# A transformer block with convolutional attention on one core: six PSUM banks for the first three rows of scores of a batch, and a first stage put in the order of its needs

## The reference

```python
x = x + conv_attn(group_norm(x))        # q, k, v = W @ x + b; softmax(q.T k) applied to v; gamma * out + x * se(x)
t = tokens(x)
a = layer_norm(t)
t = t + softmax(a @ a.T) @ a            # second attention
t = t + moe(layer_norm(t))              # 8 experts, the 2 best of a router's softmax
```

## Time and profile before

| | us |
|---|---|
| median of 3 runs (lowest to highest) | 2839.08 (2837.59 to 2839.95) |
| the profiled execution | 2836.02 |
| its span | 2834.2 |
| PE busy, matmuls | 2636.5 (93%) |
| DVE busy | 2161.3 (76%) |
| ACT busy | 2023.1 (71%) |
| POOL busy | 446.9 (16%) |
| one maximum of a chunk (DVE, L818), mean of 720 | 0.633 |

### The profile page before, as it was taken

One profiled execution on the slowest core, in us unless ns is written; L12 is line 12 of the kernel. 1 busy time (PEld: TensorE's weight loads), 2 busy tenths in 40 slices (PEclk: granted clock), 3 DMA queues, 4 the chain that ended last, 5 costly groups with the idle time before them and its releaser, 6 DMA issues.

```text
span 2834.2 us, 45738 instructions
## 1 busy us (share of the span) xinstructions
PE 2636.5 (93%) x15334; PEld 2381.2 (84%) x15334; DVE 2161.3 (76%) x5499; ACT 2023.1 (71%) x4305; POOL 446.9 (16%) x840
## 2 busy tenths in 40 slices
PE   5999989999899998999989999999999999999996
PEld 4888978889788897889978898888988889888895
DVE  4886778787787877877778777887777877788775
ACT  2777767677676876768767687676867768677774
POOL 0000210032100331003200133001220022200223
PEclk7999999999999999999999999999999999999997
DMA  1000000000000000000000000000000000000000
GB/s 35 1 1 18 7 6 1 18 7 6 7 1 18 7 6 7 1 18 7 9 4 1 18 7 11 2 1 18 10 9 1 1 21 6 9 1 1 4 9 12
DMA packets 10037, 23.05 MB, mean 8 GB/s; under 512 B 1992, under 2 KB 8528, under 8 KB 8784
## 3 DMA queue, kind: packets, MB, share of 16 engines
q1 hardware_dynamic: 9808, 20.14, 2.0%
HBM read 10.70 MB, written 9.44 MB: 7 GB/s over the span
## 4 chain that ended last, share of the span: by engine, by line
PE 61%; DVE 23%; ACT 9%; issue 5%; POOL 2%; SPq 0%; DMA 0%; ACTq 0%; DVEq 0%; POOLq 0%
PE ps L1005 17%; PE ps L1007 17%; PE ps L1006 17%; PE ps L1018 9%; DVE mx L818 6%; DVE pt_lo L828 3%; DVE pt_lo L902 3%; ACT pt_hi L612 2%; ACT p_rows L600 2%; DVE u_tok L879 1%; ACT p_rows L647 1%; POOL u_rs L518 1%; ACT pt_hi L656 1%; ACT p_rows L681 1%; DVE acc L984 1%
## 5 line engine op out<-in xcount | busy, mean ns | idle before, releaser
L612 ACT ACTIVATE pt_hi<-ps 128x384 fp32r<-128x384 f32 x864 | 425.4, 492 | 319.2 <-PE ps L1018 313.5
L828 DVE TENSOR_TENSOR pt_lo<-ps,pt_hi 128x384 fp32r<-128x384 f32 x864 | 479.5, 556 | 178.7 <-ACT pt_hi L612 170.3
L600 ACT ACTIVATE p_rows<-ps,negmax 128x512 f32<-128x512 f32 (+1 forms) x720 | 464.8, 647 | 72.9 <-DVE negmax L822 65.8
L902 DVE TENSOR_TENSOR pt_lo<-p_rows,pt_hi 128x768 fp32r<-128x768 f32 x432 | 413.9, 959 | 124.1 <-ACT pt_hi L656 122.4
L818 DVE TENSOR_REDUCE mx<-ps 128x1 f32<-128x512 f32 (+1 forms) x720 | 442.0, 633 | 79.4 <-PE ps L1007 55.4
L1018 PE MATMUL ps<-ident,p_rows 128*128 128x128 f32 x2736 | 455.7, 275 | 40.4 <-DVE pt_lo L828 22.9
L647 ACT ACTIVATE p_rows<-ps,shift 128x768 f32<-128x768 f32 x432 | 389.6, 902 | 119.1 <-PE ps L1007 114.0
L1018 PEld LDWEIGHTS ps<-ident,p_rows 128*128 128x128 f32 x2736 | 332.4, 140 | 153.8 <-issue 54.9
L656 ACT ACTIVATE pt_hi<-p_rows 128x768 fp32r<-128x768 f32 x432 | 365.6, 846 | 40.1 <-PE ps L1007 0.7
L1005 PE MATMUL ps<-pt_hi,v_hi 128*128 128x384 f32 x864 | 358.6, 415 | 2.5 <-ACT y_out L621 2.5
L1005 PE MATMUL ps<-xt_hi 128*128 128x384 f32 x864 | 305.2, 353 | 0.0
(11 more groups left out here) (165 smaller groups left out, 5162.4 us busy)
## 6 DMA issues: line engine op xcount, KB each, us to landing
x_chan<-x SPq DMA_DIRECT2D x8, 1152.0 KB, 5.1
y<-y_out SPq DMA_DIRECT2D x48, 192.0 KB, 1.9
p_rows<-ew SPq DMA_DIRECT2D x1, 512.0 KB
p_rows<-eb SPq DMA_DIRECT2D x1, 512.0 KB
p_rows<-wq SPq DMA_DIRECT2D x1, 64.0 KB
p_rows<-wk SPq DMA_DIRECT2D x1, 64.0 KB
p_rows<-wv SPq DMA_DIRECT2D x1, 64.0 KB
w_sb<-w SPq DMA_DIRECT2D x2, 4.0 KB
```

Of the source, the lines that this page charges most:

```text
L600: act.activation(p_rows[:, ROW_BUFFER[r, n % 2], a:a + w], ps[:, c, 0:w], ACT.Exp, bias=negmax[:, r % 2:r % 2 + 1], accum_out=dparts[:, n, ...
L612: act.activation(pt_hi[:, slot, :], ring_bank(step)[:, 0:BW], ACT.Copy)\
L828: dve.tensor_tensor(pt_lo[:, slot, :], ring_bank(step)[:, 0:BW], pt_hi[:, slot, :], ALU.subtract).then_inc(pt_lo_ready, 1)
L902: dve.tensor_tensor(p1_lo[:, w % 3, :], p1_f[:, w % 2, :], p1_hi[:, w % 3, :], ALU.subtract).then_inc(p1_lo_ready, 1)
```

## The change

Scores: in block 0 of each batch the fifteen chunks go round banks 0 to 5, so chunk c of row r is in bank (5 r + c) modulo 6. From block 1 on it is bank c again. Each chunk waits for the Exp that last read its bank; for block 1, row 0 these are chunks 2, 3 and 4 of row 2 (banks 0, 1, 2), chunk 4 of row 1 (bank 3) and chunk 0 of row 2 (bank 4). `pv` of tile 0 waits for chunk 1 of row 2 (bank 5). The maxima get two sets of columns, used by turns. The order of the steps in `attention0` stays as it was.

First stage: x comes in three thirds, each with a semaphore, in every batch. The weights for Q, K and V come in one transfer, the per-channel vectors in one, the two small matrices in one, the expert weights with the router's in one, their biases in one. ACT rounds the three weight matrices, DVE takes the residual behind `gn_mean`. After `gn_var` the normalisation of the first third begins. The squeeze-excite chain, five of the V projections, the folding (now steps `fold` and `foldsplit` in the ring) and the three `base` stand in slots between the scores of block 0 of batch 0. V 0 stands in slot 0, before the first chunk. The staging of the folding moves to other buffers.

```diff
+def score_bank(n, r, c):
+    return (len(QC) * r + c) % 6 if n == 0 else c
+
+def bank_before(n, r, c):
+    if n:
+        i = n * TPB + r - 1
+        if i >= TPB:
+            return i // TPB, i % TPB, c
+        i = max(i for i in range(TPB * len(QC)) if i % 6 == c)
+    else:
+        i = len(QC) * r + c - 6
+    return (0, i // len(QC), i % len(QC)) if i >= 0 else None
...
-def first_stage(b):
-    s = statistics(b) + normalise(b)
-    s += [(step[0], b, step[1]) for slot in sorted(PROJECT_SLOTS) for step in PROJECT_SLOTS[slot]]
-    return s + [step for j in range(NT) for step in attention0(b, 0, j)]
+def first_stage():
+    s = statistics(0)[:9]
+    s += [("xgnorm", 0, 0), ("xg", 0, 0), ("xgnorm", 0, 1), ("kproj", 0, 0), ("xg", 0, 1), ("kproj", 0, 1), ("xgnorm", 0, 2),
+          ("kproj", 0, 2), ("xg", 0, 2), ("qproj", 0, 0), ("kproj", 0, 3), ("kproj", 0, 4), ("kproj", 0, 5)]
+    rest = {1: [("gn_norm", 0)], 2: [("se_in", 0)], 3: [("se_out", 0)], 5: [("fold", 0, 0)], 7: [("fold", 0, 1), ("base", 0, 0)],
+            9: [("fold", 0, 2)], 11: [("foldsplit", 0)], 13: [("base", 0, 1)], 15: [("base", 0, 2)]}
+    merge(rest, {slot: [("vproj", 0, m)] for m, slot in enumerate([0, 2, 4, 8, 12, 16])})
+    merge(rest, {j: attention0(0, 0, j) for j in range(NT)})
+    return s + [step for j in range(NT) for step in rest[j]]
...
+            load(0, 0)
+            sp.dma_start(w_stage[:, :, :], wqkv).then_inc(qkv_loaded, 16)
+            load(0, 1)
+            load(0, 2)
+            sp.dma_start(biases[:, 0:4], channel).then_inc(biases_loaded, 16)
+            sp.dma_start(se_sb[:, :], se).then_inc(se_loaded, 16)
+            sp.dma_start(fold_b, eb).then_inc(fold_loaded, 16)
+            sp.dma_start(fold_w, ew).then_inc(fold_loaded, 16)
...
-            act.wait_ge(w_split, W_SPLITS)
+            act.wait_ge(qkv_loaded, 16)
+            act.activation(w_hi[:, :, :], w_stage, ACT.Copy).then_inc(w_hi_ready, 1)
+            act.wait_ge(biases_loaded, 16)
...
+                elif kind == "foldsplit":
+                    act.wait_ge(bias_folded, 1)
+                    act.activation(rw_pair[:, 0, :], rw_stage, ACT.Copy).then_inc(e_hi_ready, 1)
+                    act.activation(ew_hi[:, :], ew_stage, ACT.Copy).then_inc(e_hi_ready, 1)
...
+                    if not b:
+                        dve.wait_ge(w_hi_ready, 1)
+                        dve.tensor_tensor(w_lo[:, :, :], w_stage, w_hi[:, :, :], ALU.subtract).then_inc(w_lo_ready, 1)
+                        dve.wait_ge(biases_loaded, 16)
+                        dve.tensor_tensor(biases[:, 4:5], biases[:, 2:3], biases[:, 3:4], ALU.mult).then_inc(w_lo_ready, 1)
+                elif kind == "fold":
+                    a, z = FOLD_PARTS[step[2]]
+                    dve.wait_ge(ring_full, filled(step))
+                    dve.tensor_tensor(fold_b[:, a:z], fold_b[:, a:z], ring_bank(step)[:, 0:z - a], ALU.subtract)\
+                        .then_inc(bias_left, 1)
+                elif kind == "foldsplit":
+                    dve.wait_ge(bias_left, len(FOLD_PARTS))
+                    dve.scalar_tensor_tensor(out=fold_w, in0=fold_b, scalar=1.0 / C, in1=fold_w, op0=ALU.mult,
+                                             op1=ALU.add).then_inc(bias_folded, 1)
+                    dve.wait_ge(e_hi_ready, 2)
...
                 elif kind == "xgnorm":
                     u = step[2]
+                    if u == 0:
+                        dve.wait_ge(gn_rstd_ready, at(gn_rstd_ready, "gn_var", b))
...
-                    row = n * TPB + r
-                    if row:
-                        pe.wait_ge(p_rows_ready, at(p_rows_ready, "exp", b, (row - 1) // TPB, (row - 1) % TPB, c))
-                    elif b and c < 4:
+                    before = bank_before(n, r, c)
+                    if before:
+                        pe.wait_ge(p_rows_ready, at(p_rows_ready, "exp", b, *before))
+                    elif b and r == 0 and c < 4:
...
-                    three(ps[:, c, 0:w], q_hi[:, n % 2, tile], q_lo[:, n % 2, tile], k_hi[:, a:a + w],
+                    three(ps[:, score_bank(n, r, c), 0:w], q_hi[:, n % 2, tile], q_lo[:, n % 2, tile], k_hi[:, a:a + w],
...
+                            pe.wait_ge(p_rows_ready, at(p_rows_ready, "exp", b, *bank_before(1, 0, 5)))
```

More of the change, by code:

```diff
@@ L176, in batch @@
     return s
-PLAN = first_stage(0) + [step for b in range(B) for step in batch(b)]
+PLAN = first_stage() + [step for b in range(B) for step in batch(b)]
 RAISES = {
@@ L183 @@
     "se_in": ["ring_full", "se_hidden_ready"], "se_out": ["ring_full", "se_exp_ready"],
+    "fold": ["ring_full", "bias_left"], "foldsplit": ["bias_folded", "e_hi_ready", "e_split"],
     "xgnorm": ["xg_norm_ready"], "xg": ["xg_hi_ready", "xg_lo_ready"], "base": ["base_done"],
@@ L198 @@
 }
[L200 removed]
+LAST = {"fold": "bias_left", "gn_dev": "gn_dev_ready", "gn_var": "gn_var_ready", "se_in": "se_hidden_ready", "se_out": "se_exp_ready",
         "kproj": "k_lo_ready", "vproj": "v_lo_ready", "baset": "base_tok_ready",
@@ L383, in build @@
         y_chan_ready = signal("y_chan_ready")
-        x_loaded = signal("x_loaded")
-        w_loaded = signal("w_loaded")
+        x_loaded = [signal(f"x_loaded{i}") for i in range(LB)]
+        qkv_loaded = signal("qkv_loaded")
+        biases_loaded = signal("biases_loaded")
+        se_loaded = signal("se_loaded")
+        fold_loaded = signal("fold_loaded")
         consts_made = signal("consts_made")
-        column_sums = signal("column_sums")
         bias_left = signal("bias_left")
         bias_folded = signal("bias_folded")
-        w_split = signal("w_split")
+        e_hi_ready = signal("e_hi_ready")
+        e_split = signal("e_split")
+        w_hi_ready = signal("w_hi_ready")
+        w_lo_ready = signal("w_lo_ready")
         vector_chain = signal("vector_chain")
         y_stored = [signal(f"y_stored{i}") for i in range(2)]
-        signals = {s.name: s for s in (base_tok_ready, k_lo_ready, expert_added, terms_ready, gn_dev_ready, gn_var_ready,
+        signals = {s.name: s for s in (base_tok_ready, k_lo_ready, bias_left, expert_added, terms_ready, gn_dev_ready, gn_var_ready,
                                        logit_max_ready, o_added, o1_added, pt_lo_ready, q_lo_ready,
@@ L437, in _, with load @@
         def _(sp):
[L438 to L451, removed]
+            def load(b, u):
+                cols = slice(u * LW, (u + 1) * LW)
+                sp.dma_start(x_chan[:, cols], x[b][:, cols]).then_inc(x_loaded[u], 16)
+            load(0, 0)
[6 more added lines that the diff above has]
+            sp.dma_start(fold_w, ew).then_inc(fold_loaded, 16)
             def store(b, mb):
@@ L459, in _ @@
                     sp.wait_ge(ring_full, filled(("baset", b, NB - 1)))
-                    sp.dma_start(x_chan[:, :], x[b + 1]).then_inc(x_loaded, 16)
+                    for u in range(LB):
+                        load(b + 1, u)
                 if b:
@@ L562, in take @@
                     act.wait_ge(ring_full, filled(step))
+                    if m == 0 and not b:
+                        act.wait_ge(e_split, 2)
                     if m == 0 and b:
@@ L599, in take @@
                         act.wait_ge(ring_full, filled(("pt", b, n - 1, last_tile(c))))
-                    act.activation(p_rows[:, ROW_BUFFER[r, n % 2], a:a + w], ps[:, c, 0:w], ACT.Exp,
+                    act.activation(p_rows[:, ROW_BUFFER[r, n % 2], a:a + w], ps[:, score_bank(n, r, c), 0:w], ACT.Exp,
                                    bias=negmax[:, r % 2:r % 2 + 1],
@@ L702, in _ @@
         def _(dve):
-            dve.wait_ge(w_loaded, 16 * N_WLOADS)
             dve.wait_ge(consts_made, 12)
[L706 to L725, removed]
             def take(step):
@@ L768, in take @@
                     dve.wait_ge(se_exp_ready, at(se_exp_ready, *step))
+                    if not b:
+                        dve.wait_ge(w_lo_ready, 2)
                     link(dve.tensor_scalar(se_tmp, se_e, 1.0, None, ALU.add))
@@ L1036, in take @@
                         .then_inc(ring_full, 1)
+                elif kind == "fold":
+                    a, z = FOLD_PARTS[step[2]]
+                    pe.wait_ge(fold_loaded, 32)
+                    wait_ring(step)
+                    pe.matmul(ring_bank(step)[:, 0:z - a], ones[:, :], fold_w[:, a:z], start=True, stop=True)\
+                        .then_inc(ring_full, 1)
                 elif kind == "se_in":
                     wait_ring(step)
+                    if not b:
+                        pe.wait_ge(se_loaded, 16)
                     pe.wait_ge(se_in_ready, at(se_in_ready, "gn_norm", b))
@@ L1054, in take @@
                     pe.wait_ge(xg_lo_ready, at(xg_lo_ready, "xg", b, m // 2))
+                    if not b and not m:
+                        pe.wait_ge(w_lo_ready, 1)
                     wait_ring(step)
@@ L1153, in take @@
                     m = step[2]
+                    if not b and not m:
```

(1 more changed line is left out.)

54 lines of the change are left out of this document (26 added, 28 removed).

## The result

| | before (with one run more) | after |
|---|---|---|
| median, us (lowest to highest) | 2838.41 (2837.59 to 2839.95) | 2874.0 (2871.69 to 2874.7) |
| ratio to before, 95% interval | | 1.0123 (1.0106 to 1.0141) |
| span of the profiled execution | 2834.2 | 2872.2 |
| granted clock, mean | 0.984 | 0.975 |

The account below looks back on a forecast made before the run. TensorE, busy 36.8 of 38 us from 402 to 440 us, was taken as the bound. Terms -19.3 - 2.3 + 35.6 + 5 = +19 on 2836.0 gave 2855, with 3.1 for the median 2858; range 2841 to 2872.

Parts of the forecast that it names:

- part 5: Clock at the return to five banks: four dips more of 1.3 us, +5 us; bounds -4 to +16.
- Part 1: First stage of batch 0 up to the first scores: scores start at 25.4 us, -29.3 us.
- Part 2: Work put between the rows of batch 0: +10.0 us, leaving -19.3 us for the third row's Exp.
- Part 3: Rows of batches 1 to 7: row 1 gains 0, row 2 gains 0.33 us each, -2.3 us in all.
- The rule that bubbles mean too little PSUM: Skill's rule on bubbles: all sixteen rows 1 and 2 would gain from a sixth bank; trace agreed for batch 0 alone.
- Part 4: Return to five banks at block 1: a circle of chunk, transpose, pt_hi, Exp costs 4.45 us per batch, +35.6 us.
- The fourth rival: Clock falls in every circle: +16 in place of +5, first stage only -14; 2874 us; chance 0.15.
- The first and third rivals: First: the 4.45 us circle is given back, 2818, chance 0.07. Third: sixth bank pays everywhere, 2811, chance 0.03.
- The second: Cover and clock are kind: first stage -23.5, no dip added, circle at 3.3 us; 2840 us; chance 0.10.

Follow-up runs that it names:

- the run with banks in order: Changed kernel with chunk c in bank (c + 3) modulo 5 from block 1 on, order of steps untouched; 2817.2 us, ratio 0.9927.
- the run with the old first stage: Kernel before with the six banks alone, keeping its own loads and first stage; 2897.24 us, ratio 1.0203.
- filler: Changed kernel with useless matmuls in TensorE's idle times, ten before tile 0 and six behind each of tiles 0, 1 and 2; 2842.84 us, ratio 1.0015.
- filler in this gap: Changed kernel with bank (c + 3) modulo 5 from block 1, ten useless matmuls before tile 0 and ten before the store's transpose; 2806.19 us, ratio 0.9886.
- the run with five banks: Changed kernel's new first stage with the five banks of the kernel before; 2819.94 us, ratio 0.9934.
- the Exp first: Changed kernel with the Exp of chunks 2, 3 and 4 of block 0's last row ahead of the first transposed tile; 2842.62 us, ratio 1.0014.
- the run with five banks and filler: New first stage with five banks, plus ten useless matmuls before the store's transpose and ten before tile 0; 2818.74 us, ratio 0.9934.

## Why the prediction was wrong in its size

The sign and the mechanism were right: slower, by a circle at the return to five banks. The time, 2874, lies 2 us above the range and 16 above the forecast. The step that failed is the clock, part 5; the other parts came close.

**Part 1, up to the first scores.** -29.3 forecast, -27.6 measured (27.12). The step that was off is the load: the last third of x was not there at 6 us but at about 7.2, and the aggregate came at 8.29 and not at 6.9. From the first K projection to the scores it took 12.9, forecast 12.7.

**Part 2, the rows of batch 0.** Forecast 11.6, 6.7 and 9.7 us, measured 8.7, 6.5 and 9.0. Row 0 had been priced at half clock; by the durations of its matmuls PE was back at 2.4 GHz from about 30 us on. In sum -21.3 against -19.3, inside its bounds; the run with banks in order, where PE got there earlier, has the -23.5 that the prediction gave for full clock through row 0.

**Part 3.** Row 1 of later batches: no gain, right (7.75 against 7.76 in batch 1). Row 2: 5.59 for 5.96, -0.37; forecast -0.33, of which the prediction shows the source of 0.26 only. The rule that bubbles mean too little PSUM held in batch 0, where the run with the old first stage shows 0.67 for row 1, and not for row 1 of the others. In row 2 of the later batches PE did stand 2.70 us for a bank, and the sixth bank gave 0.37 of it.

**Part 4, the circle.** 4.45 per batch forecast; 4.49 measured, some 0.2 of it filler, once filler keeps the clock up. Nothing of it was given back later: the time from block 1's first Exp to the next batch's first one is unchanged (323.0 to 323.5 us, before 323.1 to 323.3).

**Part 5, the clock, is the step that failed.** It stood as +5 net, with +16 as its bound, "2 us at each of eight places". Measured: 31.3 in the returns (122.9 against 91.6 with filler), less 3.3 by which the rows of batches 1 to 7 fell further than part 3 had it (5.6 for 2.3, slow rows 2 among them) and less the 1.6 that one return of before had already: about +26.5. Two things were wrong in it. I priced a dip by one row's 1.28. But there PE is only part of the path; in the circle each round holds a chunk (1.42 from its start to the transpose, 0.77 at full clock) and a transpose up to pt_hi (0.88, 0.53 at full clock), a full us more per round. And I took four dips, where all eight returns had one, and it lasted through all three rounds. PE stood still for the last time before 397.91, and was granted 0.50 until 402.

**The rivals.** The fourth rival (clock down in every circle) named the right cause and gave 2874; that its number fits is chance, as it took the first stage at -14 and the clock at +16, where -21 and +26.5 were measured. With the measured clock and first stage in their places my sum gives 2858 + 21.5 - 2 = 2878. The 4 us left over are mostly the 3.1 that I added for the distance of the median from the profiled execution; after the change there is none (2874.0 and 2873.95). The first and third rivals (nothing of the circle remains) are out by the returns. The second, with no dip added, is out by its clock.

What remains open: why the low clock falls in row 1 of some batches and not of others (7.75, or up to 9.3, in one kernel). The gap before the store's transpose is 2.50 us in all of them. The runs show that filler in this gap ends the slow rows 1, and that without it their number differs from kernel to kernel.

## What to carry to other kernels

When a rotation over buffers ends and a fixed layout begins, write down for each buffer which consumer frees it, and where that consumer stands in its engine's queue; a wait on a later one than before can close a circle through two in-order queues even though no engine got more work. Renaming the buffers, so that the first tiles after the rotation take those that come free first, added no wait here and was worth 57 us against the changed kernel. Where a wait leaves TensorE idle again and again, price the whole chain at its low clock as well, for then every round gets longer, and not just the first.

## What the runs showed of the hardware

Before tile 0, TensorE's clock mostly survived a gap of 1.80 us and fell after each of 2.5. With five banks PE stood 1.76 to 1.80 there in all eight batches of the trace of before, with one slow return (8.52), and in batches 1 to 7 of the run with five banks, again with one (8.55). In the run with banks in order it stood 2.49 or 2.50 in batches 1 to 7 and 3.06 in batch 0, and all eight returns were slow. A part of an engine's time saved right before a wait so came back as a slower clock behind it: 1.4 us per batch in the run with banks in order, nearly four times the 0.37 that the sixth bank gained in row 2. Ten matmuls of no use in that gap bought it back.

The length of the gap alone does not decide. Before the store's transpose PE stood 2.50 us in all seven later batches of every kernel without filler there, and row 1 was slow in two of the seven with banks in order, and in all seven with the Exp first. The 2.70 us in row 2, in the run with five banks and filler, was in all seven batches, and four rows 2 were slow.

The load of ACT's tables, 1.28 us, stood on the path before the first Exp, that of the squeeze-excite chain, in the kernel before (first row). In the changed one (second row) it runs while ACT waits for the weights; the rounding of the weights and, without a second load in the whole trace, every Exp ran behind it:

```profile
27.95 1.28 ACT L532 ACT_TABLE_LOAD   x1 [27.95 <-PE ps L1045]
...
0.78 1.28 ACT L550 ACT_TABLE_LOAD   x1 [0.78 <-PEq L1251]
```

The Trainium skill (ScalarE: Activation LUTs, section Table sets: the hidden batching unit) says that cheap functions such as copy are in every set. By that rule a copy put first can bring Exp's table along, if the compiler picks Exp's set for it, and the trace agrees: one load, at 0.78 us, for all copies and Exp.
